# A one-core language-model tower: the Newton steps of the head norms' roots on GpSimd, a reordered prologue, and a new order of work on every engine

## The reference, cut to what matters

```
h = layernorm(fuse(emb[ids], window_mean(pca[ids]) @ proj_w + proj_b)) * g + b
X = layernorm(h);  K = X
Q = rms_norm_per_head(X @ Wq.T) * qw;   V = rms_norm_per_head(X @ Wv.T) * vw
h = h + sum over earlier tokens of Q.K * V        # linear attention, causal, no softmax
x = layernorm(h)
h = h + bitlinear(silu(conv3(bitlinear(x, w1))), w2)   # int8 activations, ternary weights
rms_norm(x) = x * rsqrt(mean(x*x) + 1e-8)
```

## Time and profile before

| | |
|---|---|
| median of 3 runs | 229.19 us (228.47 to 230.38) |
| the profiled execution's own time | 231.42 us |
| its span, first to last instruction | 229.6 us |
| mean granted TensorE clock | 0.918 of full speed |
| VectorE busy | 191.0 us, 509 instructions |
| ScalarE busy | 162.8 us, 305 instructions |
| GpSimd busy | 101.5 us, 244 instructions |
| TensorE busy | 190.4 us, 1566 instructions |

### The profile page before, as it was taken

The page is one execution under the profiler, slowest core; times in us unless marked ns, Lnnn a source line. Parts: engine busy times, 40 slices in busy tenths (PEclk is TensorE's granted clock), DMA queues, the critical chain, the costliest instruction groups (busy, mean ns, idle before and its releaser), DMA issues.

```text
span 229.6 us, 5134 instructions
## 1 busy us (share of the span) xinstructions
PE 190.4 (83%) x1566; PEld 138.8 (60%) x1566; DVE 191.0 (83%) x509; ACT 162.8 (71%) x305; POOL 101.5 (44%) x244
## 2 busy tenths in 40 slices
PE   7649797799997987999998989889788948288963
PEld 4226574568775675786586668667666635155842
DVE  3392615898979998999999999999999998858971
ACT  2632437336253997879898998999889999947712
POOL 4000150691670957556767941592463472410200
PEclk9755569979999999999999999999999997959999
DMA  6994002031223113401411340250032211201011
GB/s 134 283 365 180 3 0 46 5 65 26 47 40 77 25 21 64 92 15 26 81 36 30 60 102 0 66 108 16 1 91 49 42 51 37 59 0 46 0 49 46
DMA packets 29420, 14.25 MB, mean 62 GB/s; under 512 B 15632, under 2 KB 28114, under 8 KB 29394
## 3 DMA queue, kind: packets, MB, share of 16 engines
q1 hardware_dynamic: 27632, 13.16, 24.1%
q10 hardware_dynamic: 1762, 0.76, 1.5%
HBM read 5.51 MB, written 2.10 MB: 33 GB/s over the span
## 4 chain that ended last, share of the span: by engine, by line
DVE 30%; issue 20%; PE 20%; POOL 12%; DMA 7%; ACT 6%; SPq 3%; ACTq 1%; DVEq 1%; POOLq 0%
DVE hid L1241 4%; PE PY L907 3%; DVE ST L1184 3%; DVE h L1280 3%; POOL hid L466 2%; DMA qw_s<-in_qw_dram 2%; SPq L303 2%; DMA xsT<-xs 2%; PE PS L835 2%; PE PH L875 2%; DVE xs L1227 2%; POOL h L442 2%; DVE mx L1247 1%; ACT hid L607 1%; PE PA L786 1%
## 5 line engine op out<-in xcount | busy, mean ns | idle before, releaser
L875 PE MATMUL PH<-xsT,w1q 128*128 128x256 f16 x256 | 38.8, 278 | 15.2 <-DVE hid L1241 9.8
L466 POOL TENSOR_TENSOR hid<-hid,tap 128x508 f32<-128x508 f32 x30 | 33.3, 1112 | 37.7 <-DVE hid L1241 37.7
L607 ACT ACTIVATE hid<-PH,cb_s,cw_x 128x256 f32<-128x256 f32 x64 | 37.3, 583 | 13.0 <-PE PH L875 12.5
L875 PEld LDWEIGHTS PH<-xsT,w1q 128*128 128x128 f16 x256 | 22.4, 101 | 28.5 <-issue 16.2
L835 PE MATMUL PS<-QP,KM 128*128 128x256 f32 x128 | 34.3, 398 | 3.9 <-DMA QP<-QT 2.7
L1241 DVE SCALAR_TENSOR_TENSOR hid<-PH,cw_x,hid 128x254 f32<-128x254 f32 x64 | 30.2, 476 | 1.7 <-ACT tap L611 1.6
L611 ACT ACTIVATE tap<-PH,cw_x 128x256 f32<-128x256 f32 x60 | 29.2, 486 | 0.0
L835 PEld LDWEIGHTS PS<-QP,KM 128*128 128x128 f32 x128 | 22.6, 194 | 10.2 <-issue 4.9
L855 PE MATMUL PO<-VD,ST 128*64 128x32 f32 x512 | 25.6, 223 | 0.0
L855 PEld LDWEIGHTS PO<-VD,ST 128*64 128x64 f32 x512 | 23.3, 137 | 0.0
L442 POOL TENSOR_TENSOR h<-h,o 128x256 f32<-128x256 f32 x16 | 11.7, 740 | 25.3 <-DVE o L1196 25.3
(11 more groups left out here) (207 smaller groups left out, 412.1 us busy)
## 6 DMA issues: line engine op xcount, KB each, us to landing
QP<-QT SPq DMA_DIRECT2D x32, 64.0 KB, 2.1
VD<-Vn SPq DMA_DIRECT2D x32, 64.0 KB, 2.1
out_dram<-y SPq DMA_DIRECT2D x7, 256.0 KB, 2.4
ids_b<-in_ids_dram SPq DMA_DIRECT2D x4, 256.0 KB, 6.4
mask_b<-in_mask_dram SPq DMA_DIRECT2D x4, 256.0 KB, 7.8
w_s<-in_w1T_dram SPq DMA_DIRECT2D x1, 1024.0 KB, 9.9
w_s<-in_w2T_dram SPq DMA_DIRECT2D x1, 1024.0 KB, 12.3
fusw_s<-in_fusw_dram ACTq DMA_DIRECT2D x2, 256.0 KB, 3.0
```

The lines of the kernel that those rows point to most:

```text
L466: nc.gpsimd.tensor_tensor(part, part, tap[:, c % 2, :, 0:T - 1, :].rearrange("p u t j -> p u (t j)"), ALU.add).then_inc(tap0_ok, 1)
L607: ins = nc.scalar.activation(hid[:, c, :, :, j % 2].rearrange("p u t -> p (u t)"), hidps(j), ACT.Identity, bias=cb_s[:, j:j + 1], scale=cw ...
L875: ins = nc.tensor.matmul(hidps(j), w1q[:, k, j * 128:(j + 1) * 128], part[:, s, :, k, :], start=(n == 0), stop=(n == 2 * KC - 1))
```

## The change

**The roots.** `root_half` is gone. `root_seed` stays on VectorE. The three Newton steps move to GpSimd, in four operations each: square, times `ms`, times -0.5 plus 1.5 (`root_weight`), times the root. All operate on 128x64 numbers and each waits for the one before. `root_c` counts 13 for a group instead of 10, and `mean_q` and `scale_mean_v` wait until the last `root_error` of the group before has read `ms`.

```diff
+            def root_square(g, n):
+                wait(pool, root_c, 13 * g + 4 * n + 1)
+                nc.gpsimd.tensor_tensor(step_s[:, :], root[:, :], root[:, :], ALU.mult).then_inc(root_c, 1)
+            def root_error(g, n):
+                wait(pool, root_c, 13 * g + 4 * n + 2)
+                nc.gpsimd.tensor_tensor(step_s[:, :], step_s[:, :], ms[:, :], ALU.mult).then_inc(root_c, 1)
+            def root_weight(g, n):
+                wait(pool, root_c, 13 * g + 4 * n + 3)
+                nc.gpsimd.tensor_scalar(step_s[:, :], step_s[:, :], -0.5, 1.5, ALU.mult, ALU.add).then_inc(root_c, 1)
+            def root_step(g, n):
+                wait(pool, root_c, 13 * g + 4 * n + 4)
+                nc.gpsimd.tensor_tensor(root[:, :], step_s[:, :], root[:, :], ALU.mult).then_inc(root_c, 1)
...
             def mean_q(g):
                 wait(dve, sumq_ps, g + 1)
                 wait(dve, e8_ok, g + 1)
+                wait(dve, root_c, 13 * (g - 1) + 11)
...
-            def root_half(g):
-            def root_square(g, n):
-            def root_error(g, n):
-            def root_step(g, n):
```

```diff
             sp.dma_start(projb_s[:, :], projb).then_inc(ld_pb, 16)
-            load_tokens(0)
+            sp.dma_start(fusb_s[:, :], fusb).then_inc(ld_tab, 16)
             sp.wait_ge(zero_ok, 2)
             sp.dma_start(emb_s[:, :, 1:1 + V], embT.rearrange("(k p) v -> p k v", p=128)).then_inc(ld_tab, 16)
             sp.dma_start(pca_s[1:1 + PCA, 1:1 + V], pcaT).then_inc(ld_tab, 16)
-            sp.dma_start(fusb_s[:, :], fusb).then_inc(ld_tab, 16)
+            load_tokens(0)
...
-                    wait(sp, vd_zero, 4)
+                    wait(sp, vd_zero, 2 * g + 2)
...
+            act.wait_ge(ld_lnb, 16)
+            nc.scalar.activation(lnb_c[:, :], lnb_r[:, :], ACT.Copy, scale=-1.0 / D, accum_out=lnb_m[:, :]).then_inc(lnb_c1, 1)
+            act.wait_ge(lnb_c1, 1)
+            nc.scalar.activation(lnb_c[:, :], lnb_r[:, :], ACT.Identity, bias=lnb_m[:, :]).then_inc(lnb_ok, 1)
...
-            keep_warm(20, PY[:, 0:UT])
+            keep_warm(24, PY[:, 0:UT])
...
+            keep_warm(6, PY[:, 0:UT])
...
-            keep_warm(4, PY[:, 0:UT])
+            keep_warm(3, PY[:, 0:UT])
...
-            keep_warm(5, PY[:, 0:UT])
+            keep_warm(4, PY[:, 0:UT])
...
             dve.wait_ge(pool_c, 11)
-            dve.wait_ge(ld_qw, 16)
...
-            for step in range(7):
+            for step in range(5):
                 features(0, step)
...
+            for step in range(5, 7):
+                features(0, step)
...
+            dve.wait_ge(ld_qw, 16)
+            for k in range(KC):
+                nc.vector.tensor_scalar(identq[:, k, :], ident[:, :], qw_s[:, k:k + 1], None, ALU.mult)
+                ins = nc.vector.tensor_scalar(bdmask[:, k, :].rearrange("p (h e) -> p h e", h=8),
+                                              heads[:, :, None].to_broadcast([128, 8, DH]), qw_s[:, k:k + 1], None, ALU.mult)
```

367 lines of the change are left out of this document (170 added, 197 removed).

## The result

The changed kernel takes 232.79 us (median of 4 runs, 231.58 to 233.94) against 229.47 us (228.47 to 230.38) for the kernel before: a ratio of 1.0145 with a 95% interval of 1.0077 to 1.0213. It is slower by about 1.5%. The forecast was 221.1 us with a range of 215 to 228. Some executions of every kernel here, the one before included, are longer by some per cent whatever the code, and the ratios leave them out. The profiled execution of the changed kernel took 232.74 us with a span of 231.0 us, against 231.42 and 229.6 us. That is 1.3 us more, where the medians differ by 3.3: the profiled execution of the kernel before lay 1.95 us above its median.

The account below looks back on a forecast made before the run. VectorE was taken to set the pace from 82.6 to 196.9 us, chains of short steps before. Prologue -4.6, two chains +2.5 each, -1.2, -1.7 and dense stage -5.6 made -8.1: 229.2 to 221.1 us, range 215 to 228.

Parts of the forecast that it names:

- The early chains: Root chains on GpSimd, seed to scale_v: 5.1 us with handovers, exposed in groups 0 and 1, +2.5 us each.
- the stretch between: Between keys_queries(0) and group 3's root seed: -1.2 us from warmed keys and queries, -1.7 us from VectorE's freed queue.
- warming calls: Matmuls ahead of group 1's keys and queries, which ran cold: both halves faster, -1.2 us.
- VectorE's freed time: Roots of groups 0 to 2, 7.8 us, leave VectorE's queue before the dense stage: 1.7 us won (bounds 0 and 4).
- The prologue: Start to keys_queries(0): -3.9 for an earlier first mean, -0.3 for features, -0.4 for the clock, together -4.6 us.
- the tokens' landing at 8.7 us: In the opening, VectorE waits for the tokens, taken to land at 8.7 us (bounds 4 and 9.1).
- The dense stage: From group 3's root seed to the last xs_low, 82.6 to 196.9 us: ScalarE becomes next bound, -5.6 us.
- VectorE's relief: Root steps leaving VectorE: 2.61 us a group, 13.0 us in the five groups of the dense stage.
- The end: From the last xs_low on, same order and no roots: 0 us, plus or minus 0.5.
- the third: Rival: root chains in GpSimd's queue hold back add_tap and residual in the five dense groups, 234.1 us; chance 0.12.
- The second rival: All of VectorE's relief passed on in the dense stage, prologue gains more from an early clock: 216.5 us; chance 0.18.
- The first rival: None of VectorE's relief passed on in the dense stage: 226.7 us, 228 with late tokens; chance 0.20.

Follow-up runs that it names:

- the filler experiment: 24 more matmuls of the warm tile where TensorE stands idle, added to the changed kernel: ratio 1.004 to the kernel before.
- the three repairs: The changed kernel with the tokens' load early on SyncE, 24 filler matmuls and scale_taps() right behind clip_w(1): ratio 0.982 to the kernel before.
- the last test of the chain's length: The kernel with the three repairs, with two Newton steps instead of three in all groups: ratio 0.9794 to the kernel before.

## Why the prediction was wrong, step by step

The forecast was -8.1 us and the spans differ by +1.4, which is 9.5 us apart: 6.4 of them in the stretch of the first three groups, 2.4 in the dense stage, 2.1 in the prologue, and -1.4 at the end.

- **The early chains.** The prediction had a chain of 4.9 us, 5.1 with its handovers, exposed in groups 0 and 1 at +2.5 us each. The size was about right: 5.42, 5.98 and 5.11 us in groups 0 to 2, at 0.33 us an operation and a pitch of 0.40 where nothing drew them out. The count was not: it is three groups, +2.4, +3.4 and +1.9, together 7.6 us more from seed to `scale_v` where the sum had 5.0. I had rows for groups 0, 1 and 4 and none for group 2, where it was 3.26 us before.
- **The clock.** The prediction took the clock as something to be won back in the stretch between (-1.2 by warming calls) and put the loss of it at nothing. This term and the missing third chain are the steps that turned a gain into a loss. The longer chain left TensorE idle for 1.59 us ahead of `gram(3)`, and 10 us at half clock followed: 2.85 us by the filler experiment, 2.4 us on the whole run by its ratio. `keys_queries(2)` ran cold instead of `keys_queries(1)`, whose first half took 0.70 us now against the 1.23 of the earlier trace rows. The term had the right mechanism for one group, and the change moved the cold spell to the next.
- **The offsets.** The -1.2 of the warming calls and the 1.7 us for VectorE's freed time don't show after the change: outside the chains the early part was 0.2 us longer than before. The half clock hid them, as far as one trace shows: with the clock at 1.00 in the kernel with the three repairs, the same pieces were 3.5 us shorter than before, against the 2.9 of the two terms. Whether it was VectorE's freed time or the new order that gave them isn't shown.
- **The prologue.** -2.5 instead of -4.6. The step that failed is the tokens' landing at 8.7 us: the first `mask_p` was at 11.03, past the upper bound of 9.1 that I had set, as it was in all eleven kernels with this load late. Two steps fewer ahead of the mean did their part (14.12 us against 15.92). With the load ahead of the two table loads the mask was at 8.59 and `keys_queries(0)` at 28.7, which is what the sum had said (about 29).
- **The dense stage.** -3.2 instead of -5.6. The term that was mis-sized is VectorE's relief. The prediction added up durations, 5 x 2.61 = 13.0 us, and since that is more than the 9.4 us of ScalarE it made ScalarE the next bound. VectorE's busy time in the stage fell by 6.7 us only, from 111.38 to 104.69. In the old list the steps stood between other calls, and there an operation starts before the one ahead has ended, so that a step of 0.22 us held the queue for 0.13:

```profile
100.72 0.22 DVE L1152 TENSOR_TENSOR step_s<-step_s,half 128x64 f32<-128x64 f32 x1
100.85 0.48 DVE L1241 SCALAR_TENSOR_TENSOR hid<-PH,cw_x,hid 128x254 f32<-128x254 f32 x1
101.25 0.22 DVE L1156 SCALAR_TENSOR_TENSOR root<-step_s,root 128x64 f32<-128x64 f32 x1
101.38 0.42 DVE L1263 TENSOR_REDUCE hmax<-PY 128x2 f32<-128x256 f32 x1
```

  So less than 9.4 us left VectorE, it stayed 94.2% busy, and 3.2 of the 6.7 us were passed on. ScalarE came to 95.0%, near the 96.5% foreseen, which looks like the reason given and isn't: take 7 us from ScalarE and nothing moves.
- **The end.** -1.4 instead of 0, with 0.5 allowed. The clock there was 0.84 against 0.90, so it isn't that; the lists differ a little. No run tests it.
- **The rivals.** The time came out nearest the third (234.1), by another mechanism: under the new lists four operations less in each group moved the rest by 1.2 us only, and `silu` and the second norm waited for GpSimd for 1.9 and 0.3 us. Under the old lists the same move costs 10.5%, with its longest waits at `scale_v` and some 9 us of waits of the kind that this rival named. The factor of two that the Trainium skill gives for GpSimd (page GPSIMD Engine Reference, section Engine selection) was not met at this size: 0.33 us against VectorE's 0.25 to 0.28.
- **Slips in its sums**, without weight in the forecast. For group 0 its own rows give 5.1 - 3.06 = 2.0 us, not 2.5. The second rival speaks of 1 us more in the prologue and adds 0.8. The first rival's 228 with late tokens should be 229.3 by the bound of -2.

In sum: -2.5 in the opening, +7.8 in the early part, -3.9 in the rest make the +1.4 us of the span. Of the +7.8, 3.5 came back with the three repairs, at a clock of 1.00 throughout. The other 4.3 are a chain 7.8 us longer less 3.5 us won around it. That is a division of one trace and no experiment: hurrying `scale_v` in the list made the time worse, and the last test of the chain's length was disturbed by the clock, so how much a shorter chain would give back stays open.

## What to carry to other kernels

Work moved off the fullest engine, when it is part of a chain of steps that others wait for, is paid at the chain, at the full length of what is exposed, and once more by the granted clock if the wait leaves TensorE idle; so look at how long TensorE stands idle behind the moved step, for every group that goes through it, and cost the clock as a loss before you count the relief. Count the relief by what the steps add to the engine's busy time, not by the sum of their durations: 13.0 us by the one were 6.7 by the other. A list order and the placement of an operation belong together: one without the other cost 5.6 and 10.5% here. When an engine is called the bound, take some work from it and see whether the time moves; a busy share of 95% on ScalarE was no bound here.

## What I had not expected of the hardware

- A GpSimd operation on 64 numbers takes 0.33 us with two inputs, 1.3 times VectorE's 0.25, and 0.26 us as tensor-scalar. The same operation took 1.20 us when it started 0.17 us behind a 1.22 us int8-to-f16 copy on VectorE (rows of group 1 above), and 0.73 us beside a feature step in group 0.
- The half clock lasted 10 us although TensorE was busy for nearly all of it, which I would have taken for enough to bring it back. It lasted as long in each of the six kernels without the filler. The window of the changed kernel:

```profile
61.20:71.20 10.00, 9.74 (x50) 7.54 (x50) 4.86 (x13) 3.81 (x7) 5.13 (x21) 0.50 0.27 54
```

- The same opening ended between 29.15 and 32.13 us in eleven profiles, so a term of 2 us there needs more than one profile.
- Two operations of VectorE that don't wait for each other overlap in the trace: the next starts 0.1 us or so before the one ahead ends (rows of the dense stage above), so short operations cost its queue less than their durations.
